# Cross scores by two heads per product, attention tails by query tile, and new merged orders of two threads in a two-layer decoder kernel

## What is computed

```python
x = _layernorm(x + _L0_attn_ref(x, ...))         # gated linear attention, 4 heads
x = _layernorm(x + _L0_xattn_ref(x, ctx_768, ...))   # cross attention, 16 heads of 16, 77 keys
x = _layernorm(x + _L0_ffn_ref(x, ...))          # 8 experts, top 2
x = _layernorm(x + _L1_attn_ref(x, ...))         # windowed self attention, 16 heads of 16, +-128 keys
x = _layernorm(x + _L1_xattn_ref(x, ctx_768, ...))   # cross attention, scores clipped at +-10000
x = _layernorm(x + _L1_ffn_ref(x, ...))          # 8 experts, top 2, with capacity
```

## Time and profile before

| what | value |
|---|---|
| times of three runs | 1130.4, 1131.32, 1134.64 us; median 1131.32 us |
| span of the profiled execution | 1131.2 us |
| TensorE busy | 1010.0 us (89%) |
| VectorE, ScalarE, GpSimd busy | 618.1, 425.0, 255.4 us |
| mean granted TensorE clock | 0.967 |

### The profile page before, as it was taken

How to read it: one execution, slowest core, us unless ns; L and a number is a source line. 1 busy time by engine, 2 the same in 40 slices (tenths; PEclk the granted TensorE clock), 3 DMA queues, 4 the chain that set the end, 5 groups by cost and what they waited for, 6 DMA issues and landing times.

```text
span 1131.2 us, 20802 instructions
## 1 busy us (share of the span) xinstructions
PE 1010.0 (89%) x8612; PEld 719.1 (64%) x8612; DVE 618.1 (55%) x1398; ACT 425.0 (38%) x557; POOL 255.4 (23%) x282
## 2 busy tenths in 40 slices
PE   6889889999987899999998798879888987986997
PEld 3666566576575799997445465747565665654566
DVE  2653753662667564333334846675575668765443
ACT  1533533524433355555541254142416231541112
POOL 0310310120130233333322020231013110210662
PEclk9999999899897899999999899999999999997999
DMA  6013413211400691111113000200020010004447
GB/s 188 1 43 126 135 43 107 89 43 44 152 1 1 254 378 57 47 48 47 43 39 98 1 2 6 85 2 5 1 76 2 6 38 1 1 2 131 130 135 236
DMA packets 64237, 80.50 MB, mean 71 GB/s; under 512 B 12736, under 2 KB 57680, under 8 KB 63120
## 3 DMA queue, kind: packets, MB, share of 16 engines
q1 hardware_dynamic: 53392, 61.15, 16.3%
q0 software_dynamic: 5664, 15.47, 4.2%
q10 hardware_dynamic: 5088, 2.56, 0.9%
HBM read 46.13 MB, written 33.03 MB: 70 GB/s over the span
## 4 chain that ended last, share of the span: by engine, by line
PE 61%; DVE 17%; ACT 12%; issue 5%; DMA 2%; POOL 2%; SPq 0%; ACTq 0%; DVEq 0%; POOLq 0%
PE ps L1522 8%; PE ps L1857 7%; DVE sb_arena L874 6%; ACT sb_arena L645 6%; PE ps L1658 5%; PE ps L1680 4%; PE ps L1885 4%; PE ps L1868 3%; PE ps L1728 3%; PE ps L1783 3%; DVE sb_arena L878 3%; PE ps L1566 2%; PE ps L1995 2%; PE ps L1630 2%; PE ps L1905 2%
## 5 line engine op out<-in xcount | busy, mean ns | idle before, releaser
L645 ACT ACTIVATE sb_arena<-ps 77x2048 f32<-77x2048 f32 (+1 forms) x64 | 116.5, 1880 | 27.9 <-PE ps L1612 26.7
L1388 POOL TENSOR_TENSOR sb_arena<-sb_arena,sb_neghalf 128x2 f32<-128x2 f32 x40 | 28.7, 719 | 397.2 <-DVE sb_arena L840 397.2
L1522 PE MATMUL ps<-sb_arena,sb_wreg 128*128 128x256 f32 (+1 forms) x512 | 110.8, 365 | 6.8 <-issue 3.8
L1522 PEld LDWEIGHTS ps<-sb_arena,sb_wreg 128*128 128x128 f32 (+1 forms) x512 | 89.0, 195 | 23.7 <-issue 8.3
L1857 PE MATMUL ps<-sb_arena 128*128 128x128 f32 x800 | 100.2, 280 | 3.2 <-ACT sb_arena L757 2.3
L1630 PE MATMUL ps<-sb_arena 32*77 32x256 f32 (+1 forms) x1024 | 78.4, 424 | 25.8 <-ACT sb_arena L645 13.1
L1857 PEld LDWEIGHTS ps<-sb_arena 128*128 128x128 f32 x800 | 97.0, 196 | 5.2 <-ACT sb_arena L757 2.9
L757 ACT ACTIVATE sb_arena<-sb_arena 128x1024 f32 x72 | 76.0, 1057 | 16.8 <-issue 12.4
L1630 PEld LDWEIGHTS ps<-sb_arena 32*77 32x77 f32 (+1 forms) x1024 | 44.3, 177 | 46.1 <-ACT sb_arena L645 24.2
L874 DVE TENSOR_REDUCE sb_arena<-ps 128x8 f32<-128x2048 f32 x32 | 71.0, 2282 | 3.5 <-PE ps L1586 3.5
L1566 PE MATMUL ps<-sb_headrow,sb_identb 128*32 128x512 bf16 (+1 forms) x266 | 65.8, 385 | 1.4 <-DVE sb_arena L878 1.3
(11 more groups left out here) (285 smaller groups left out, 1886.9 us busy)
## 6 DMA issues: line engine op xcount, KB each, us to landing
sb_arena<-in_m_w SPq DMA_DIRECT2D x8, 1536.0 KB, 9.8
sent<-sb_xres SPq DMA_DIRECT2D x32, 256.0 KB, 2.6
sb_arena<-outs SPq DMA_DIRECT2D x16, 512.0 KB, 6.0
outs<-sb_zeros SPq DMA_DIRECT2D x4, 1664.0 KB, 9.7
sent<-sb_zeros SPq DMA_DIRECT2D x2, 2560.0 KB, 13.7
sb_arena<-in_m_w SPq DMA_DIRECT2D x16, 256.0 KB, 3.4
early<-sb_xres SPq DMA_DIRECT2D x12, 256.0 KB, 2.9
sb_arena<-in_xT SPq DMA_DIRECT2D x8, 256.0 KB, 3.2
```

Of the source, the lines that this page charges most:

```text
L645: nc.scalar.activation(dst, src, ACT.Exp).then_inc(S(f"h_PT{p}"), 1)
L1522: ins = mm(dst[:, m * cols:(m + 1) * cols], wt[0:rows, k, m * P:(m + 1) * P], src[0:rows, k, 0:cols], start=(k == 0), stop=(k == KC - 1))
```

## The change

1. A cross score unit is 2 chunks x 4 row tiles = 8 products with 154 key columns (the even and the odd masked copy side by side) in place of 16 with 77. The four unread products behind B's first unit go.
2. The tails are split. `values` and `OT` come in two halves (groups 0, 1 and 2, 3); `untr`, `norm`, `tout`, `onT`, `wo`, `res` come once for each query tile. Banks change with it: `turned_bank` (bank 2 or 1) and `result_bank` (bank 3 or 2). Stage `g_keys` of the next pair now waits for the residual of this one, since it writes bank 2. The first `bn_stats` follows its own half of the residual.
3. The merged order is written out for whole layers, not for each pair, in turns of 1 to 8 stages. The threads can so drift against each other by a few stages. In pairs 0 and 1 of layer 0 `q` of B moves behind the first score unit of A (in the last pair it stood there already), in its pairs 0 and 2 `nmT` of B moves ahead of the first `ST` of A, in its pair 2 `g_keys` of B follows straight on B's last `wo`, and other neighbours trade places; the S1 scores and exponentials still alternate A, B, A, B as before.
4. Routing pieces move. In layer 0's last pair the `table` goes from ahead of `norm` A to behind it; `perm` is signalled rather than waited for. In layer 1 `count` moves from behind `v` of A to behind `v` of B, `place` from ahead of `o_turn` to behind the last `o_route`. The other unread products stay; those ahead of the last `o_turn` first wait for A's residual.

```diff
 def after_probs(c):
-    return [(n, c) for n in ("values", "OT", "untr", "norm", "tout", "onT", "wo", "res", "rstd", "final")]
+    out = []
+    for i in range(2):
+        out += [("values", c, i), ("OT", c, i)]
+    for n in (("untr", "norm"), ("tout", "onT"), ("wo", "res")):
+        for t in range(NT):
+            out += [(x, c, t) for x in n]
+    return out + [("rstd", c), ("final", c)]
...
-TURNS0 = (3, 3, 4, 2, 3, 4, 2, 3, 4, 2, 3, 4, 5, 7, 4, 1, 2, 4, 4, 4, 2, 1, 4, 4, 1, 2, 2, 2, 2, 2, 2, 2, 2, 1, 2, 7, 6, 3, 5, 4)
...
+EXTRA0 = {(1, 2, "o_logits"): ["choose"], (0, 3, "g_mix"): ["count"], (0, 3, "k", X0): ["counts"], (0, 3, "g_turn"): ["rank"],
+          (0, 3, "untr", X0, 0): ["hots"], (1, 3, "values", X0, 0): ["table"], (1, 3, "OT", X0, 1): ["index"],
+          (1, 3, "untr", X0, 0): ["place", "raw"], (0, 3, "wo", X0, 1): ["turned"], (1, 3, "res", X0, 0): ["first"],
+          (0, 3, "store"): ["blocks", "gather"]}
+EXTRA1 = {(1, 3, "q", S1): ["choose"], (1, 3, "v", S1): ["count"], (0, 3, "scores", S1, 0): ["counts"], (1, 3, "exp", S1, 0): ["rank"],
+          (1, 3, "OT", S1, 0): ["hots"], (1, 3, "o_route"): ["place"]}
...
+            def heads(p, n, c, i):
+                act.wait_ge(S(f"h_OT_done{p}"), 2 * c.at(n) + i + 1)
+                nc.scalar.activation(bufs[p].OT[:, 2 * i:2 * i + 2, :], halves(bank(p, 2 + i)), ACT.Copy).then_inc(S(f"h_OT{p}"), 1)
...
+                v.reciprocal(b.rec[:, t, :], o[:, :, DH]).then_inc(S(f"h_on{p}"), 1)
...
+                v.tensor_tensor(b.res[:, t, :], result_bank(p, t), b.xb[:, t, :], ALU.add).then_inc(S(f"h_res{p}"), 1)
...
                 else:
-                    for g in range(G):
+                    for k in range(KC):
                         for r in range(RT):
-                            ins = mm(bank(p, r)[:, g * M:(g + 1) * M], b.q[rows_of(r), g // 2, u * P:(u + 1) * P], kz[rows_of(r), g // 2, g % 2, :],
-                                     start=(g == 0), stop=True, skip_group_check=True)
-                    if p == 1 and u == 0:
-                        ins = idle(p, IDLE_SCORES, 0, G * M)
+                            ins = mm(bank(p, r)[:, 2 * k * M:2 * (k + 1) * M], b.q[rows_of(r), k, u * P:(u + 1) * P],
+                                     kz[rows_of(r), k, :, :].rearrange("p a m -> p (a m)"), start=(k == 0), stop=True, skip_group_check=True)
...
+                if n:
+                    pe.wait_ge(S(f"h_res{p}"), NT * X0.at(n))
```

More of the change, by code:

```diff
@@ L147, in self_head, with in_turns @@
     return [(n, c) for n in ("turn", "xinT", "k", "kz", "q", "qe", "v", "va")]
-def lockstep(n, stages):
-    return [(s, p, n) for s in stages for p in range(2)]
-def in_turns(n, threads, turns, extra):
+def in_turns(threads, turns, extra):
     out, at = [], [0, 0]
@@ L187, in first_thread, with whole_thread @@
         of_pair(n, "o_turn", "o_T") + of_pair(n + 1, "g_decay", "g_z") + of_pair(n, "o_route", "o_logits", "store")
-def first_layer():
-    out = lockstep(0, [("g_keys",), ("g_low",), ("g_decay",), ("g_z",)])
-    for n in range(PAIRS):
-        extra = {(1, "g_sp"): ["choose"], (0, "g_mix"): ["count"], (0, "g_y"): ["counts"], (1, "g_y"): ["rank"],
-                 (1, "split", X0): ["hots", "table"], (0, "tout", X0): ["place"], (0, "onT", X0): ["raw"], (0, "wo", X0): ["turned"],
-                 (1, "norm", X0): ["index"], (0, "rstd", X0): ["first"], (1, "final", X0): ["blocks"], (1, "store"): ["gather"]} if n + 1 == PAIRS else {}
-        out += in_turns(n, [first_thread(p, n) for p in range(2)], LAST0 if n + 1 == PAIRS else TURNS0, extra)
-    return out
+def whole_thread(head, thread, p):
+    return head + [(stage, m) for n in range(PAIRS) for stage, m in thread(p, n) if m < PAIRS]
+LAST = PAIRS - 1
+EXTRA0 = {(1, 2, "o_logits"): ["choose"], (0, 3, "g_mix"): ["count"], (0, 3, "k", X0): ["counts"], (0, 3, "g_turn"): ["rank"],
[4 more added lines that the diff above has]
+          (1, 3, "OT", S1, 0): ["hots"], (1, 3, "o_route"): ["place"]}
+def first_layer():
+    head = of_pair(0, "g_keys", "g_low", "g_decay", "g_z")
+    return in_turns([whole_thread(head, first_thread, p) for p in range(2)], TURNS0, EXTRA0)
 def second_thread(p, n):
@@ L777, in _ @@
             act.wait_ge(S("rescaled"), 3)
-            play(head1, stages)
-            for order in order1:
-                play(order, second)
+            play(order1, second)
             picks(3, 4)
@@ L1309, in _ @@
             scale_bias(["s1_bq", "x1_bq"], "rescaled")
-            play(head1, stages)
-            for order in order1:
-                play(order, stages | routing(1))
+            play(order1, stages | routing(1))
             choose_late(1)
@@ L1475, in store1 @@
                     unread(p)
[L1477 to L1479 removed]
+            play(order1, stages | {"store": lambda p, n: store1(p, n)})
             def gather1(e):
```

188 lines of the change are left out of this document (92 added, 96 removed), and 16 rows, old and new, of tables (TURNS0, TURNS1).

## The result

The changed kernel takes 0.38% more time than the kernel before: ratio 1.0038, 95% interval 1.0024 to 1.0052, 20 runs of each. Its median is 1133.85 us (1129.68 to 1142.19) against 1130.64 (1125.38 to 1134.64). Beside the experiments it ran twice more, in other sets, with ratios of 1.0051 (1.0015 to 1.0087) and 1.0012 (0.9988 to 1.0036). So it costs 1 to 6 us where 16 us less had been forecast.

The account below looks back on a forecast made before the run. TensorE, 89% busy, was taken to bound the kernel by its work, 121 us without work, and its clock. Gains 2.1 + 1.5 + 5.4 + 6.0 + 1.1 = 16.1 us from 1131.2 gave 1115 us, range 1103 to 1131.

Parts of the forecast that it names:

- Step 1: Cross score product: a unit falls from 1.03 to 0.73 us, gaining on seven phases' first units, 2.1 us (0 to 3.6).
- The other estimate: Cross score product bound by its weight loads: halving them halves the unit, giving 3.6 us in place of 2.1.
- that same shadow: Behind a phase's first cross score unit, three maxima back to back for 4.21 us, hiding TensorE's work there.
- Step 2: Order in X0: 0.5 us new in pair 1, 1.0 at pair 0's start, together 1.5 us (-1 to 3).
- Step 3: Split tails: 10.1 us from waits gone, less 4.7 of fixed eviction costs, gives 5.4 us (-9 to 10).
- a sign of being wrong: In the tails: new waits on VectorE at `untr` or `tout` would show the prediction wrong; no size given.
- Step 4: Last pair of layer 0: scores A0 to `ST` A 4.1 us shorter, plus some lost clock, 6 us (0 to 10).
- that cover: Layer 0's last tail: TensorE's `tout` A, `values` B, `wo` A, `untr` B, some 8 us, during the 5 us `table`.
- Step 5: `count` in layer 1: moved behind `v` of B, its 1.10 us wait for `choose` goes, 1.1 us gained.
- Rival (a): Cross phases: TensorE's clock falls more often, costing 16 us, all of the gain: 1131 us; chance 0.12.
- The argument against it: Against the clock falling in cross phases: 2.66 of 5 us busy from 745 left the clock at 1.00.
- Rival (b): Split tails: all 19.0 us of fixed costs on the path and the 10.1 us of waits stay: 1139.5 us; chance 0.08.

Follow-up runs that it names:

- before_no_fillers: The kernel before with only the four unread products behind B's first cross unit taken out: 0.72% slower than before, 6.7 us by the medians.
- late_start: both_with_fillers_2 with only the changed kernel's start (g_keys, g_low, g_decay, g_z of A ahead of B's): 1.0007 of before.
- new_layer0_old_layer1: The changed kernel with unread products kept, B's g_keys back ahead of A's g_decay, and before's order in layer 1: 0.9925 of before.
- split_alone: The kernel before with only its tails split, halves directly behind each other in before's order, old score product and unread products kept: 0.41% faster than before.
- product_with_fillers: The kernel before with only the new cross score product, the four unread products kept: 0.63% faster than before.
- old_layer0_fillers: The changed kernel with before's order and routing places in layer 0 and the unread products kept: 0.9949 of before.
- start_and_fillers: The changed kernel with B's g_keys back ahead of A's g_decay and the four unread products put back: 1132.6 us, 0.9951 of before.
- both_with_fillers_2: The kernel before with the new score product and split tails, before's order and unread products kept, run a second time: 0.9938 of before.
- late_start_filled: late_start with ten unread products in TensorE's wait between A's g_keys and g_decay: 0.9968 of before.

## Why the prediction failed

**Step 1** held in its size. The new unit is 0.74 us (157.98 to 158.72, 46 ns a record; 0.73 was taken). From the first unit to `ST` of A it is 6.87 us, 0.33 less than in the earlier trace rows. The other estimate went by the price of a weight load in the Trainium skill ("TensorE: Matmul & The Clock Gate", "LDWEIGHTS (loading the stationary operand)"), which goes by its columns alone, and would have halved the unit with its loads. The trace disagrees: the loads halve and the unit keeps 72%. What failed is the step's last sentence, "The removed fillers stand in that same shadow and are worth nothing in time." They cost next to nothing (0.08 us a phase) but hold the clock: before_no_fillers is 0.72% slower. That alone, 6.7 us, is more than steps 1 and 2 were to win (3.6).

**Step 2** failed twice. The start was taken as 1.0 us of gain; it costs 7.9 us in late_start, 4.9 of waiting and some 3 of lost clock. The step looked at threads and not at ScalarE's queue, where the weight loads stood in the page of before just as now. In pair 1 the forecast from the first projection to the first `ST` was 14.4 us; new_layer0_old_layer1 has 15.54 at full clock (154.30 to 169.84), the old order with the new product 14.91 (150.52 to 165.43). The working left out the four unread products between scores B1 and `nmT` (1.04 us). So the new order costs 0.6 us there, and 2.3 us over the whole cycle of pair 1, where step 2 had put the neighbours' moves at 0.

**Step 3** held in the old order: split_alone is 4.6 us faster (2.5 to 6.8), 5.4 was forecast. Its parts don't agree as well: by the cycles layer 1 gives 1.7 us in pairs 0 and 1 (102.9 to 101.2, full clock) and layer 0 costs 0.6 in pair 0 (86.1 in product_with_fillers, 86.7 in old_layer0_fillers). The fixed costs were sized fairly (VectorE +8.8, ScalarE +9.8 us busy for 11 and 8); that a quarter of them is bare isn't shown. The waits at `wo` went (5.7 to 0.3 us), as forecast. In the new order others came on VectorE: `tout` from 3.9 to 5.4 us, which the prediction had named as a sign of being wrong, and `turn` from 2.0 to 7.2, which it had not.

**Step 4** hit its first half: 7.5 us from scores A0 to `ST` of A for the 7.6 forecast. The second half failed: the 7.7 us gained until `values` are given back in the tail (8.4 us more). The sentence "should that cover fail, the 5 us appear ahead of `norm` B" names only a smaller part of it, the 2.3 us of waits behind `table`; the same waits stand in start_and_fillers. The largest part, 4.0 us, is the clock, which the step took as a gain ("Adding some of the lost clock") and which moved from the scores into the tail. With less of it lost the same order does better: in start_and_fillers the stretch from scores A0 to the experts takes 41.9 us (335.28 to 377.22) against 46.6 in the changed kernel, 45.8 before and 44.0 in both_with_fillers_2. start_and_fillers and both_with_fillers_2 lose about as much clock in it (2.1 and 2.7 us, summed as in the table of cycles), so the order itself is worth 2 us here, and low clock hides it.

**Step 5** held: the 1.10 us ahead of `count` in layer 1 are gone. (A wait at the same line in the last experts also fell, from 3.39 to 1.68 us; nothing in the change aimed at it.)

**What was not costed**: X1 in pair 2 of layer 1, 3.5 us, and pair 0 there, 0.9 us, both under what the description of the change called "other neighbours trade places".

**The base** of the sum was a span, 1131.2 us, where the forecast is a time. In the runs the time lies 1.7 to 2.1 us above its span, so this execution took about 1133. It did no harm, as before's median over 20 runs is 1130.64.

**The rivals.** Rival (a), the clock falls more often, was given 0.12 and had the sign right. The clock is the largest single cause, but not the whole: the fillers taken out cost 3 to 8 us in five pairs of kernels, and the clock behind the start some 3, where (a) named 16. That its 1131 us lies near the measured 1133.85 is in part luck, since the wait at the start and the orders made up the rest. Of its two reasons, the removed fillers hold; the shorter products don't, as product_with_fillers has a clock of 0.974. The argument against it rested on one stretch with few products at full clock; the granted clock depends on more than the stretch itself, as the same phases fall in one run and not in another. The Trainium skill's statement ("TensorE: Matmul & The Clock Gate", "Part 1: The HAM clock gate (the "warmup" mystery)") that activity releases the throttle stood in the prediction, but the sum was left without it: before_no_fillers and late_start_filled agree with it, 6.7 us lost by leaving unread work out and about 4 won by adding some. Rival (b), bare halves, is excluded by split_alone for the old order.

**The account**, in parts of before's time: new code with fillers -0.65%, fillers taken out +0.2 to +0.7% (five pairs of kernels), start +0.7%, X1 of pair 2 +0.3%. The sum is +0.55 to +1.05%; the changed kernel has +0.1 to +0.5%. So the account doesn't close. The parts were measured in different kernels. The new order of layer 0 wins back 0.9 us in pair 0 and 2 in the last pair, and loses 2.3 in pair 1, which is about even; the rest isn't split further. Start and fillers together won 0.6% in the changed kernel, less than the two alone. Why the clock falls in one phase and not in its twin isn't shown.

## What to carry to other kernels

Unread products that stood in a wait were not dead weight here, to clear away with a shorter product. Take them out alone first and look at the clock of many runs, not at one profile. Before an order is changed at the start of a kernel, read the issuing engine's queue: here an eviction stood behind 19 us of DMA issues, and what waited for it could not start earlier. A gain in one stretch is worth counting only to the next fixed point (here the experts' start): of the 7.7 us won ahead of `values` nothing was left there.

## What the runs showed of the hardware

Ten unread products in a gap of 4.9 us lifted the granted clock from 0.60 to 1.00 in the window from 20 to 28 us, which holds the end of the gap, and made the kernel some 4 us faster. Four unread products of 0.52 us, eight times in a kernel, held the mean granted clock at 0.973 where it was 0.9635 without them, and cost 0.08 us a phase. A cycle at full clock repeats to 0.1 us (101.2 us in layer 1, in six traces from four sets). The spread of the changed kernel from 1130 to 1142 us goes with the clock: about 0.9 us for each 0.001 of mean granted clock, a line that takes up nine tenths of the variance of its 20 runs; in the runs of before beside the experiments it is 0.5 to 0.6 us.
